# Tile t+1's first two query/key projections and first rotation issued at the end of tile t; another first tile

## The chip, the cores and the metric

The kernel runs on one core of a Trainium2 chip. Its engines run side by side, each through its own instructions in order, and wait for each other through semaphores: TensorE (PE in the profile) multiplies, VectorE (DVE), ScalarE (ACT) and GpSimd (POOL) do the rest, SyncE (SP) issues most DMAs. The metric is the device time of one execution in microseconds; lower is better.

## The reference

One transformer layer over 4096 rows of 512 numbers in float32:

```python
qkv = x @ w_qkv.T                                  # q, k, v: 16 heads of 32
q = q * cos + rotate_half(q) * sin                 # the same for k
scores = einsum('bhqd,bhkd->bhqk', q, k) * scale
keep = (rel >= 0) & (rel < 64)                     # 64 keys back at most
attn = softmax(where(keep, scores, -inf))
x1 = layernorm(x + (attn @ v) @ w_out.T)
fuse = silu((x1 @ w_gate) * s_gate) * ((x1 @ w_up) * s_up)     # 512 -> 2048, int8 weights
out = layernorm(x1 + (fuse @ w_down) * s_down)
```

## The kernel before

The rows are cut into 8 tiles of 512, a tile into 4 blocks of 128 rows. Each engine's program is written out by hand as `first()`, a loop over `body(t, True, True)` for t = 1 to 7, and `body(8, False, True)`. `first()` does the attention of tile 0 alone; `body(t)` does the attention of tile t together with the feed-forward part (FFN) of tile t-1; the last body is the FFN of tile 7.

The attention of a tile begins with three projections for each block j: "even" and "odd" query/key columns (`project_even`, `project_odd`) and values (`project_v`), each 4 float32 products of 128x512 on TensorE, written to one PSUM bank each. The first tile uses banks 0 to 3 for all of them, so that a block's projections wait until VectorE is through with those of an earlier block. VectorE rotates (`rope_products`, 4 instructions, and `rope_sums`, 2), ScalarE rounds the result to float16 (`split_high`), VectorE takes the rest as a second float16 (`split_low`; for block 3 of the first tile GpSimd does this), and SyncE turns both by DMA transposes (`turn_qk`, two for each block) into `qkT`. Values are split in the same way (`keep_v` on ScalarE, `split_v` on VectorE) and copied (`cross_v`).

Then come 16 steps s, one for each block and group of 4 heads: `scores` (TensorE), `maxima` and `bias` (VectorE), `exponentials` (ScalarE), `weights` (VectorE), `keep_probs_high` (ScalarE), `split_probs` (GpSimd), `turn_probs` (a DMA transpose), `weigh_v` (TensorE), and for every second step `keep_o` (VectorE). In the first tile a pair of buffers takes the split probabilities, so step s's `keep_probs_high` waits until the transpose of step s-2 has landed. Output projections (`project_o`), the residual and the first layer norm (`start_x1`, `finish_x1`, with the power of -0.5 on GpSimd in `invert_deviation1`) and the split of x1 for the FFN (`split_x1_high`, `split_x1`, `turn_x1`) follow.

In `body` TensorE first makes the projections in the order E0 O0 E1 O1 V0 E2 O2 V1 E3 O3 V2 (E even, O odd, V values, with the block), then two groups of scores and V3, then the 16 gate and up products of the FFN with the steps of the attention between them, the output projections, and 4 `down` products. VectorE ends a body with the second layer norm (`start_y`, `finish_y`); before that it finds the largest x of the next tile (`tile_maximum`), which GpSimd spreads over the partitions (`spread_maximum`), and works out the next tile's scales (`next_scales`). It begins the next body with the keys that are carried over, the scaled rotation tables (`start_tables`) and the rotation of block 0.

The FFN's weights come in nine DMAs from GpSimd during the first tile's steps: eight of 512 KB after the odd steps, and `wd`, 2048 KB, after the last step. The rows of x for the residual are loaded at steps 12 to 15 (`load_rows`), the next tile's x at step 6 (`load_xT`). Ahead of `first()` VectorE takes the maxima of the query/key weights and of x for the scales, in three reductions of 2048 columns.

## Time and profile before

| | |
|---|---|
| median of 3 runs | 1273.59 us (1273.41 to 1275.9) |
| the profiled execution | 1274.88 us, its span 1273.0 us |
| TensorE busy | 1203.5 us, 95% of the span, 8200 matrix products |
| VectorE busy | 932.7 us, 73% |
| ScalarE busy | 570.1 us, 45% |
| GpSimd busy | 372.7 us, 29% |
| mean granted clock of TensorE | 0.972 of full speed |

The span is the time from the first to the last instruction of the profiled execution; 1.9 us lie around it. Busy time is the time in which an engine computes; waits, branches and the issue of DMAs are not counted. The granted clock is a share of 2.4 GHz; it has two levels, 1 and 0.5, and a mean between them tells how long each was held.

### The profile page before, as it was taken

The page shows a single profiled execution, that of the slowest core. Times are in us where ns is not written, and L with a number is a line of the kernel's source. Part 1 is how long each engine was busy: PE and PEld are TensorE (multiplying, and loading weights), DVE is VectorE, ACT ScalarE, POOL GpSimd, SP SyncE. Part 2 cuts the span into 40 slices and gives each one's busy share as a digit, 9 for nine tenths or more (in the row PEclk, how much of TensorE's full clock was granted, in tenths as well). Part 3 has the DMA queues.
Part 4 walks back from the last instruction along what each step waited for, and adds up shares of the span by engine and source line. Part 5 has one row for each costly group of instructions (what it writes and reads, how often), then busy time and mean ns, then how long its engine had stood idle before and what let it go on. Part 6 is the DMA issues. An engine that isn't in the chain of part 4 may idle for free.

```text
span 1273.0 us, 24755 instructions
## 1 busy us (share of the span) xinstructions
PE 1203.5 (95%) x8200; PEld 554.6 (44%) x8200; DVE 932.7 (73%) x2794; ACT 570.1 (45%) x1609; POOL 372.7 (29%) x379
## 2 busy tenths in 40 slices
PE   7726699999999999999999999999999999999997
PEld 3312344444444444444444444444444444444443
DVE  6655589866897579965898669975799658975543
ACT  1355048801685028820487016840288105960230
POOL 0044205611154103521055102541045210551331
PEclk9857899999999999999999999999999999999999
DMA  6577665432654245550744326542545507443000
GB/s 215 116 158 179 149 132 100 99 74 67 144 105 89 51 104 121 101 96 35 150 92 92 71 75 148 102 89 44 124 104 100 94 35 165 85 84 75 25 1 33
DMA packets 346392, 124.74 MB, mean 98 GB/s; under 512 B 309536, under 2 KB 330272, under 8 KB 346272
## 3 DMA queue, kind: packets, MB, share of 16 engines
q1 hardware_dynamic: 338160, 108.32, 41.6%
q0 software_dynamic: 3216, 6.29, 1.8%
q10 hardware_dynamic: 4896, 8.52, 1.8%
q8 instruction: 76, 1.25, 0.4%
q14 instruction: 44, 0.36, 0.1%
HBM read 27.67 MB, written 8.39 MB: 28 GB/s over the span
## 4 chain that ended last, share of the span: by engine, by line
PE 86%; DVE 4%; issue 3%; DMA 2%; SPq 2%; ACT 1%; POOL 1%; POOLq 0%; ACTq 0%; DVEq 0%
PE bank L493 59%; PE bank L603 15%; PE bank L511 8%; PE bank L570 3%; PE bank L550 2%; DMA x<-y 2%; DVE fuse L831 1%; ACT bank L735 1%; DMA xT_sb<-xT 1%; SPq L313 0%; SPq L335 0%; DVE fuse L842 0%; POOL y L418 0%; POOL fuse L440 0%; SPq L296 0%
## 5 line engine op out<-in xcount | busy, mean ns | idle before, releaser
L418 POOL TENSOR_TENSOR xT_sb<-probs,xT_sb 128x512 f16<-128x512 f32 x112 | 129.6, 1157 | 413.0 <-ACT xT_sb L693 413.0
L493 PE MATMUL bank<-x1T,wg 128*128 128x512 f16 (+1 forms) x1032 | 244.2, 380 | 2.2 <-DVE ffn_tmp L890 2.2
L735 ACT ACTIVATE bank<-bank,neg_max,qk_scale 128x128 f32<-128x128 f32 x512 | 219.8, 430 | 51.7 <-DVE neg_max L883 51.7
L493 PE MATMUL bank<-x1T,wu 128*128 128x512 f16 x1024 | 241.9, 379 | 0.0
L693 ACT ACTIVATE fuse<-fuse 128x512 f16<-128x512 f32 x128 | 70.0, 617 | 378.4 <-DVE fuse L837 378.4
L493 PE MATMUL bank<-wqkv,xT_sb 128*128 128x512 f32 x512 | 229.1, 598 | 2.0 <-DMA wqkv<-w_qkvT 2.0
L603 PE MATMUL bank<-wd,fuse 128*128 128x512 f16 x1024 | 222.3, 379 | 0.0
L423 POOL TENSOR_TENSOR fuse<-ffn_tmp,fuse 128x512 f16<-128x512 f32 x128 | 148.4, 1159 | 71.5 <-ACT fuse L693 70.2
L603 PEld LDWEIGHTS bank<-wd,fuse 128*128 128x128 f16 x1024 | 100.1, 98 | 123.2 <-issue 4.0
L493 PEld LDWEIGHTS bank<-x1T,wu 128*128 128x128 f16 x1024 | 100.2, 98 | 120.9 <-issue 0.5
L493 PEld LDWEIGHTS bank<-wqkv,xT_sb 128*128 128x128 f32 x512 | 97.2, 191 | 122.5 <-issue 118.4
L493 PEld LDWEIGHTS bank<-x1T,wg 128*128 128x128 f16 x1032 | 96.6, 98 | 118.7 <-issue 5.6
L511 PE MATMUL bank<-wqkv,xT_sb 128*128 128x512 f32 x256 | 120.4, 615 | 13.4 <-DVE v_own L847 8.1
L877 DVE CUSTOM_DVE_ANT_0 bank<-bank,mask_tile 128x128 f32<-128x128 f32 x496 | 129.0, 323 | 0.0
L703 ACT ACTIVATE ffn_tmp<-bank,tanh_scale 128x512 f32<-128x512 f32 x128 | 88.1, 689 | 78.1 <-PE bank L493 46.7
L493 PE MATMUL bank<-wout,v_own 128*128 128x512 f32 x256 | 121.3, 628 | 0.8 <-DVE v_own L867 0.8
L894 DVE SCALAR_TENSOR_TENSOR ffn_tmp<-bank,fuse_scale,ffn_tmp 128x512 f32<-128x512 f32 x128 | 96.2, 751 | 19.0 <-PE bank L493 6.7
L890 DVE SCALAR_TENSOR_TENSOR ffn_tmp<-ffn_tmp,bank 128x512 f32<-128x512 f32 x128 | 86.9, 679 | 27.3 <-ACT ffn_tmp L703 27.3
L735 ACT ACTIVATION_READ_ACCUMULATOR bank<-bank,neg_max,qk_scale 128x1 f32 x512 | 104.5, 204 | 0.0
L831 DVE TENSOR_TENSOR fuse<-bank,tables 128x512 f32<-128x512 f32 x128 | 79.4, 684 | 13.7 <-PE bank L493 10.7
L842 DVE TENSOR_TENSOR fuse<-fuse 128x512 f16<-128x512 f32 x124 | 77.3, 687 | 15.2 <-ACT fuse L693 15.2
L859 DVE SCALAR_TENSOR_TENSOR probs<-bank,inv_sum 128x512 f32<-128x512 f32 x120 | 83.0, 691 | 4.8
(109 smaller groups left out, 1101.1 us busy)
## 6 DMA issues: line engine op xcount, KB each, us to landing
xT_sb<-xT SPq DMA_DIRECT2D x36, 256.0 KB, 3.9
v_cross<-v_own SPq DMA_DIRECT2D x64, 128.0 KB, 2.7
qkT<-x SPq DMA_DIRECT2D x32, 256.0 KB, 3.6
out<-y ACTq DMA_DIRECT2D x32, 256.0 KB, 2.1
wqkv<-w_qkvT SPq DMA_DIRECT2D x2, 1024.0 KB, 7.3
wg<-w_gate POOLq DMA_DIRECT2D x4, 512.0 KB, 4.2
wu<-w_up POOLq DMA_DIRECT2D x4, 512.0 KB, 4.1
wd<-w_down POOLq DMA_DIRECT2D x1, 2048.0 KB, 11.6
```

The costliest lines, as they stand in the source:

```text
L418: done(probs_low, pool.tensor_tensor(place[:, 1, :, :], probs_place(s, ffn), place[:, 0, :, :], ALU.subtract))
L423: done(fuse_low, pool.tensor_tensor(fuse[:, s, 1, :], ffn_tmp[:, s % 2, :], fuse[:, s, 0, :], ALU.subtract))
L493: last = pe.matmul(dst, lhsT, rhs, start=(i == 0), stop=(i == len(pairs) - 1))
L511: pe.matmul(even, xT_sb[:, j, k, :], wqkv[:, k, 0:EMB], start=(k == 0), stop=(k == KC - 1))
L603: last = pe.matmul(bank32[DOWN_BANKS[j % 2]], fuse[:, s, z, rows], wd[:, s, :], start=(s == 0 and z == 0), stop=(s == STEPS - 1 and z == 1))
L703: done(tanh_done, act.activation(ffn_tmp[:, s % 2, :], bank32[2 * (s % 2)], ACT.Tanh, scale=tanh_scale[:, s:s + 1]))
L735: last = act.activation(unit, unit, ACT.Exp, bias=neg_max[:, s % 2, h // 3, h % 3:h % 3 + 1], scale=qk_scale[:, 2:3], accum_out=row_sum[:, ...
L831: last = dve.tensor_tensor(free_view(rope_t[i], heads), free_view(src, heads), table(i), ALU.mult)
L859: done(probs_ready, dve.scalar_tensor_tensor(out=probs_place(s, ffn), in0=units, scalar=2.0 ** PROB_BITS, in1=inverse, op0=ALU.mult, op1=A ...
L877: last = dve.tensor_tensor_reduce(out=unit, in0=unit, in1=mask[:, :], scale=1.0, scalar=MASKED, op0=ALU.add, op1=ALU.max, accum_out=row_ma ...
L890: done(gated, dve.scalar_tensor_tensor(out=tmp, in0=tmp, scalar=1.0, in1=bank32[2 * (s % 2)], op0=ALU.add, op1=ALU.mult))
L894: done(fused, dve.scalar_tensor_tensor(out=tmp, in0=bank32[2 * (s % 2) + 1], scalar=fuse_scale[:, s:s + 1], in1=tmp, op0=ALU.mult, op1=ALU ...
```

## The change

It has four parts. First, the projections E0, O0, E1, O1 of tile t+1 stand at the end of body t instead of at the start of body t+1, as do the carried keys, the tables and the rotation of block 0 (VectorE: `carry_keys`, `first_rope`), ScalarE's `split_high` of block 0 and the load of the tables. The loop runs over t = 1 to 6; body 7 is written out, without the next tile's maximum, its spreading, its scales and its loads. Second, `first()` spreads its projections over all eight banks, rotates block 1 into the free `x1`, makes only V0 before the scores of step 0, and puts V1 to V3 into the steps. GpSimd takes `split_low` of blocks 1, 2 and 3. Step s weighs values for step s-3 instead of s-2. Third, tile 1's E0, O0, E1, O1 stand at steps 10, 11, 14 and 15 of `first()`, the first layer norm of blocks 0 and 1 at steps 9 to 15, and tile 1's keys, tables and rotation of block 0 at its end; rows of x are loaded at step 5, the next x at step 7. The FFN's weights are issued in three DMAs (2048 KB each) when the transpose of step 15 has landed. Fourth, ahead of `first()` the maxima are taken piece by piece as the loads land (four reductions of 512 columns, one of 2048, four of 512), and the FFN's constants are prepared later.

```diff
@@
-        QKV_BANKS = 4
         V_BANKS = (4, 6, 5, 7)
+        FIRST_QK_BANKS = ((2, 3), (0, 1), (5, 6), (2, 3))
+        FIRST_V_BANKS = (7, 0, 1, 3)
+        FIRST_PROJ_BANKS = (2, 3, 6, 5)
         DOWN_BANKS = (5, 7)
...
+            return bank32[(V_BANKS if ffn else FIRST_V_BANKS)[j]]
+
+        def proj_bank(j, ffn):
+
+            return bank32[j if ffn else FIRST_PROJ_BANKS[j]]
 
...
-            with eng.Fori(1, NT) as t:
-                body(t, True, True)
-            body(NT, False, True)
+            with eng.Fori(1, NT - 1) as t:
+                body(t, True, True, True)
+            body(NT - 1, True, True, False)
...
-                cross_v(a, 1)
-                turn_qk(a, 2)
                 for s in range(STEPS):
                     turn_probs(a, s, False)
                     if s == 0:
-                        cross_v(a, 2)
-                    if s == 4:
+                        turn_qk(a, 2)
+                    if s in (2, 5):
+                        cross_v(a, (1, 2)[s // 5])
+                    if s == 6:
                         turn_qk(a, 3)
+                    if s == 5:
+                        for j in range(NB):
+                            load_rows(a, j)
+                    if s == 7:
                         cross_v(a, 3)
-                    if s == 6:
                         for j in range(NB):
                             load_xT(a + 1, j, False)
-                    if s >= STEPS - NB:
-                        load_rows(a, s - (STEPS - NB))
-
-            def body(t, attn, ffn):
+                    if s == 8:
+                        load_tables(a + 1)
+
...
-                    for j in range(NB):
-                        load_xT(a + 1, j)
+                    if more:
+                        for j in range(NB):
+                            load_xT(a + 1, j)
+                        load_tables(a + 1)
...
-                a = 0
+                a, ffn = 0, False
+                split_low(a, 1, ffn)
                 for s in range(STEPS):
-                    split_probs(a, s, False)
-                    if s % 2:
-                        load_inner(*((w_gate, wg) if s < 2 * KC else (w_up, wu)), s // 2 % KC)
-                    if s == 3:
-                        split_low(a, 3)
+                    split_probs(a, s, ffn)
+                    if s == 0:
+                        split_low(a, 2, ffn)
+                    if s == 5:
+                        split_low(a, 3, ffn)
+                    if s in (10, 14):
+                        invert_deviation1(a, s // 4 - 2)
+                pool.wait_ge(first_probsT_in[NB - 1], 16 * STEPS // NB)
+                for src, dst in ((w_gate, wg), (w_up, wu)):
+                    pool.dma_start(dst[:, :, :], src.rearrange("(k p) n -> p k n", p=P)).then_inc(wffn_in, 16)
                 pool.dma_start(wd[:, :, :], w_down.rearrange("(s p) n -> p s n", p=P)).then_inc(wffn_in, 16)
-                for j in range(NB):
+                for j in range(2, NB):
...
+            def project_even(a, j, ffn, early=False):
 
                 wait_xT(pe, a, j)
-                if ffn:
+                if early:
+                    wait(*((v_low, pe, a - 1, 1) if j == 0 else (proj_read, pe, a - 1, 0)))
+                elif ffn:
                     wait(*((proj_read, pe, a - 1, 2 * j + 1) if j < 2 else (rope_read, pe, a, j - 2)))
-                elif j >= 2:
-                    wait(v_low, pe, a, j - 2)
+                elif j == NB - 1:
+                    wait(rope_read, pe, a, 0)
...
+            def project_odd(a, j, ffn, early=False):
+
+                if early:
+                    wait(*((v_low, pe, a - 1, 2) if j == 0 else (proj_read, pe, a - 1, 1)))
+                if j == 0 and not ffn:
+                    pe.wait_ge(wq_odd_in, 16)
                 done(qk_done, qkv(j, 1, qk_banks(j, ffn)[1]))
...
-                for j in range(NB - 1):
+                for j in range(2):
                     project_even(a, j, ffn)
                     project_odd(a, j, ffn)
-                    project_v(a, j, ffn)
+                project_v(a, 0, ffn)
+                project_even(a, 2, ffn)
+                project_odd(a, 2, ffn)
                 scores(a, 0, ffn)
+                project_even(a, 3, ffn)
+                project_odd(a, 3, ffn)
                 scores(a, 1, ffn)
-                project_even(a, 3, ffn)
                 scores(a, 2, ffn)
-                project_odd(a, 3, ffn)
-                for s in range(STEPS):
-                    if 1 <= s < STEPS - 2:
+                project_v(a, 1, ffn)
+                for s in range(1, STEPS):
+                    if s + 2 < STEPS:
                         scores(a, s + 2, ffn)
-                    if s == 1:
+                    if s >= 3:
+                        weigh_v(a, s - 3, ffn)
+                    if s == 3:
+                        project_v(a, 2, ffn)
+                    if s == 6:
                         project_v(a, 3, ffn)
-                    if s >= 2:
-                        weigh_v(a, s - 2, ffn)
-                    if s in (8, 12, 15):
-                        project_o(a, (s - 7) // NG if s < 15 else 2, ffn)
+                    if s in (8, 12):
+                        project_o(a, s // 4 - 2, ffn)
+                    if s in (10, 14):
+                        project_even(a + 1, s // 4 - 2, True, True)
+                    if s in (11, 15):
+                        project_odd(a + 1, s // 4 - 2, True, True)
+                weigh_v(a, STEPS - 3, ffn)
+                project_o(a, 2, ffn)
                 weigh_v(a, STEPS - 2, ffn)
                 weigh_v(a, STEPS - 1, ffn)
                 project_o(a, NB - 1, ffn)
 
-            def body(t, attn, ffn):
+            def body(t, attn, ffn, more):
                 a, f = t, t - 1
 
                 if attn:
-                    for j in range(NB):
+                    project_v(a, 0, ffn)
+                    for j in range(2, NB):
                         project_even(a, j, ffn)
                         project_odd(a, j, ffn)
-                        if j:
-                            project_v(a, j - 1, ffn)
+                        project_v(a, j - 1, ffn)
...
                     down(f, j, attn)
+                if more:
+                    for j in range(2):
+                        project_even(a + 1, j, ffn)
+                        project_odd(a + 1, j, ffn)
...
+                split_high(a, 0, ffn)
+                split_high(a, 1, ffn)
+                exponentials(a, 0)
                 keep_v(a, 0, ffn)
-                keep_v(a, 1, ffn)
-                split_high(a, 2)
-                exponentials(a, 0)
-                keep_v(a, 2, ffn)
+                split_high(a, 2, ffn)
                 for s in range(1, STEPS):
                     exponentials(a, s)
                     keep_probs_high(a, s - 1, ffn)
-                    if s == 2:
-                        split_high(a, 3)
-                    if s == 3:
-                        keep_v(a, 3, ffn)
+                    if s in (2, 4, 8):
+                        keep_v(a, s.bit_length() - 1, ffn)
+                    if s == 5:
+                        split_high(a, 3, ffn)
+                    if s == 12:
+                        split_x1_high(a, 0)
                 keep_probs_high(a, STEPS - 1, ffn)
-                split_x1_high(a)
-
-            def body(t, attn, ffn):
+                split_x1_high(a, 1)
+                split_high(a + 1, 0, True)
+                split_x1_high(a, 2)
+                split_x1_high(a, 3)
...
+            def carry_keys(a):
+                wait(scale_chain, dve, a - 1, 7)
+                wait_qkT(dve, a - 1, NB - 1)
+                done(k_carried, dve.tensor_scalar(before, qkT[:, NB, :, WINDOW:P], carry_scale[:, :], None, ALU.mult))
+
+            def first_rope(a):
+                start_tables(a)
+                rope_products(a, 0, True)
+                rope_sums(a, 0, True)
+
...
+                    if s >= 5 and s % 2:
+                        keep_o(a, (s - 5) // 2)
                     attention_step(a, s, ffn)
-                    if s == 1:
+                    if s == 3:
                         rope_products(a, 3, ffn)
-                        rope_sums(a, 3)
-                    if s == 3:
-                        split_v(a, 3, ffn)
+                        rope_sums(a, 3, ffn)
+                    if s in (2, 5, 8):
+                        split_v(a, (s + 1) // 3, ffn)
+                    if s in (9, 13):
+                        start_x1(a, s // 4 - 2, ffn)
+                    if s in (11, 15):
+                        finish_x1(a, s // 4 - 2)
+                    if s == 14:
+                        split_x1(a, 0)
+                next_scales(a, ffn)
+                carry_keys(a + 1)
                 keep_o(a, STEPS // 2 - 2)
+                first_rope(a + 1)
+                split_x1(a, 1)
                 keep_o(a, STEPS // 2 - 1)
+                dve.wait_ge(v_setup, V_SETUP_STEPS + 1)
+                start_x1(a, 2, ffn)
+                finish_x1(a, 2)
+                start_x1(a, 3, ffn)
+                split_x1(a, 2)
+                finish_x1(a, 3)
+                split_x1(a, 3)
+                dve.reciprocal(fuse_inv[:, :], power[:, 2:3]).then_inc(fuse_inverted, 1)
                 dve.wait_ge(sdown_in, 16)
                 dve.tensor_scalar(sdown[:, :], sdown[:, :], power[:, 2:3], 2.0 ** 18, ALU.mult, ALU.mult)\
                     .then_inc(sdown_scaled, 1)
...
-                split_v(a, 0, ffn)
-                split_v(a, 1, ffn)
-                rope_products(a, 2, ffn)
...
                 finish_y(f, NB - 1)
+                if more:
+                    carry_keys(a + 1)
+                    first_rope(a + 1)
...
+            for k in range(KC):
+                dve.wait_ge(wq_even_in[k], 16)
+                dve.tensor_reduce(part_max[:, k:k + 1], wqkv[:, k, 0:EMB], AX.X, ALU.max,
+                                  apply_absolute_value=True).then_inc(setup, 1)
+            dve.wait_ge(wq_odd_in, 16)
+            dve.tensor_reduce(part_max[:, KC:KC + 1], wqkv[:, :, EMB:2 * EMB], AX.XY, ALU.max,
+                              apply_absolute_value=True).then_inc(setup, 1)
+            for j in range(NB):
+                wait_xT(dve, 0, j)
+                dve.tensor_reduce(x_max[:, j:j + 1], xT_sb[:, j, :, :].rearrange("p k t -> p (k t)"), AX.X, ALU.max,
+                                  apply_absolute_value=True).then_inc(setup, 1)
+            dve.wait_ge(setup, SETUP_MAXIMA - 2)
+            dve.tensor_reduce(largest[:, 0:1], x_max[:, :], AX.X, ALU.max).then_inc(setup, 1)
+            dve.tensor_reduce(largest[:, 1:2], part_max[:, :], AX.X, ALU.max).then_inc(setup, 1)
+            count[0] += 2
...
```

TensorE in `first()`, from the program's first product; `bank` with a number is the PSUM bank written, `wqkv,xT_sb` is a projection, `qkT` a group of scores. Before:

```order
L511 MATMUL bank0<-wqkv,xT_sb 128x512 x4
L493 MATMUL bank1<-wqkv,xT_sb 128x512 x4
L493 MATMUL bank2<-wqkv,xT_sb 128x512 x4
L511 MATMUL bank3<-wqkv,xT_sb 128x512 x4
L493 MATMUL bank0<-wqkv,xT_sb 128x512 x4
L493 MATMUL bank1<-wqkv,xT_sb 128x512 x4
L511 MATMUL bank2<-wqkv,xT_sb 128x512 x4
L493 MATMUL bank3<-wqkv,xT_sb 128x512 x4
L493 MATMUL bank0<-wqkv,xT_sb 128x512 x4
L550 MATMUL bank4<-qkT 32x128 x16
L550 MATMUL bank6<-qkT 32x128 x16
L511 MATMUL bank1<-wqkv,xT_sb 128x512 x4
```

And of the change, the same place:

```order
L534 MATMUL bank2<-wqkv,xT_sb 128x512 x4
L514 MATMUL bank3<-wqkv,xT_sb 128x512 x4
L534 MATMUL bank0<-wqkv,xT_sb 128x512 x4
L514 MATMUL bank1<-wqkv,xT_sb 128x512 x4
L514 MATMUL bank7<-wqkv,xT_sb 128x512 x4
L534 MATMUL bank5<-wqkv,xT_sb 128x512 x4
L514 MATMUL bank6<-wqkv,xT_sb 128x512 x4
L578 MATMUL bank4<-qkT 32x128 x16
L534 MATMUL bank2<-wqkv,xT_sb 128x512 x4
L514 MATMUL bank3<-wqkv,xT_sb 128x512 x4
L578 MATMUL bank6<-qkT 32x128 x16
```

The scores of step 0 (the first row with `qkT`) stand behind seven projections instead of nine, and no bank is used twice ahead of them.

TensorE at steps 10 to 12 of the first tile; `v_cross` and `v_own` are the two halves of `weigh_v`, `wout` is an output projection. Before:

```order
L550 MATMUL bank6<-qkT 32x128 x16
L570 MATMUL bank7<-x1,v_cross 32x128 x8
L570 MATMUL bank7<-x1,v_own 32x128 x8
L550 MATMUL bank5<-qkT 32x128 x16
L570 MATMUL bank7<-x1,v_cross 32x128 x8
L570 MATMUL bank7<-x1,v_own 32x128 x8
L493 MATMUL bank1<-wout,v_own 128x512 x4
L550 MATMUL bank4<-qkT 32x128 x16
L570 MATMUL bank7<-x1,v_cross 32x128 x8
```

And of the change:

```order
L578 MATMUL bank4<-qkT 32x128 x16
L598 MATMUL bank7<-x1,v_cross 32x128 x8
L598 MATMUL bank7<-x1,v_own 32x128 x8
L534 MATMUL bank0<-wqkv,xT_sb 128x512 x4
L578 MATMUL bank6<-qkT 32x128 x16
L598 MATMUL bank7<-x1,v_cross 32x128 x8
L598 MATMUL bank7<-x1,v_own 32x128 x8
L514 MATMUL bank1<-wqkv,xT_sb 128x512 x4
L578 MATMUL bank5<-qkT 32x128 x16
L598 MATMUL bank7<-x1,v_cross 32x128 x8
L598 MATMUL bank7<-x1,v_own 32x128 x8
L514 MATMUL bank3<-wout,v_own 128x512 x4
```

The two rows with `wqkv,xT_sb` are E0 and O0 of tile 1, each between the scores or weighed values of two steps.

VectorE at the end of `first()`, from `keep_o` of steps 14 and 15 on; `v_own<-bank` is `keep_o`, `fuse<-bank,tables` are `rope_products`. Before:

```order
L867 TENSOR_REDUCE v_own<-bank 128x256 x2
L1028 TENSOR_SCALAR sdown<-sdown,power 128x512
L900 SCALAR_TENSOR_TENSOR qkT<-bank,v_scale,qkT 128x512
L905 BN_STATS stats<-qkT 128x6
L907 MEMSET wait_taker 128x1
L908 BN_AGGR mean_var<-stats 128x2
L910 TENSOR_SCALAR mean_var<-mean_var 128x1
```

And of the change, from the carried keys on:

```order
L1052 TENSOR_SCALAR qkT<-qkT,carry_scale 128x16x64
L918 TENSOR_REDUCE v_own<-bank 128x256
L1032 TENSOR_SCALAR tables<-tables,qk_scale 128x256
L881 TENSOR_TENSOR fuse<-bank,tables 128x512 x4
L887 TENSOR_TENSOR fuse<-fuse 128x512
L888 TENSOR_TENSOR fuse<-fuse 128x512
L978 SCALAR_TENSOR_TENSOR qkT<-qkT 128x512
L918 TENSOR_REDUCE v_own<-bank 128x256
L952 SCALAR_TENSOR_TENSOR qkT<-bank,first_unscale,qkT 128x512
```

The carried keys, the tables and tile 1's rotation of block 0 stand around the last two `keep_o`; before, they stood 43 rows behind the last `keep_o`, inside the loop.

## Rows read from the trace of the kernel before

**Rows 1.** Page, the chain that ended last: share of the span by engine.

```profile
PE 86%; DVE 4%; issue 3%; DMA 2%; SPq 2%; ACT 1%; POOL 1%; POOLq 0%; ACTq 0%; DVEq 0%
```

**Rows 2.** Busy time by stretch (us: stretch and length; busy and count by engine; clock; DMA).

```profile
61.40:138.80 77.40, 32.83 (x485) 16.60 (x487) 38.92 (x185) 37.96 (x139) 28.38 (x29) 0.68 0.81 190
...
293.30:441.00 147.70, 147.70 (x1026) 68.19 (x1025) 114.94 (x346) 71.13 (x201) 44.63 (x46) 1.00 0.45 95
```

**Rows 3.** TensorE's timeline, first tile, front (start, length, what, idle before it).

```profile
41.05 5.69 PE L511 MATMUL bank<-wqkv,xT_sb 128*128 128x512 f32 x8 [8.11 <-DVE v_own L847]
```

**Rows 4.** VectorE's timeline, first tile, front.

```profile
16.78 2.28 DVE L1143 TENSOR_REDUCE largest<-xT_sb 128x1 f32<-128x2048 f32 x1
...
22.40 2.48 DVE L831 TENSOR_TENSOR fuse<-bank,tables 128x512 f32<-128x512 f32 x4
...
60.75 0.69 DVE L859 SCALAR_TENSOR_TENSOR probs<-bank,inv_sum 128x512 f32<-128x512 f32 x1
```

**Rows 5.** Page, groups of instructions: a group of maxima (count; busy us, mean ns; idle).

```profile
L877 DVE CUSTOM_DVE_ANT_0 bank<-bank,mask_tile 128x128 f32<-128x128 f32 x496 | 129.0, 323 | 0.0
```

**Rows 6.** The chain in order of time, front.

```profile
6.06 7.92 DMA xT_sb<-xT
```

**Rows 7.** DMA issues by line: count, KB each, median us from issue to landing.

```profile
wg<-w_gate POOLq DMA_DIRECT2D x4, 512.0 KB, 4.2
...
wd<-w_down POOLq DMA_DIRECT2D x1, 2048.0 KB, 11.6
...
qkT<-fuse SPq DMA_TRANSPOSE x64, 4.0
```

**Rows 8.** TensorE's timeline, steps and end of the first tile, start of tile 1.

```profile
67.17 0.30 PE L570 MATMUL bank<-x,v_cross 128*32 128x128 f16 x8 [1.11 <-DMA x<-y]
...
103.71 0.29 PE L570 MATMUL bank<-x,v_cross 128*32 128x128 f16 x8 [1.76 <-DMA x<-y]
...
120.20 0.29 PE L570 MATMUL bank<-x,v_cross 128*32 128x128 f16 x8 [0.89 <-DVE v_own L867]
...
138.78 0.40 PE L570 MATMUL bank<-x,v_cross 128*32 128x128 f16 x8 [8.62 <-DMA x<-y]
...
155.95 7.03 PE L493 MATMUL bank<-wqkv,xT_sb 128*128 128x512 f32 x16
...
191.16 0.41 PE L550 MATMUL bank<-qkT 128*32 128x128 f16 x16
```

**Rows 9.** The timelines of GpSimd and of SyncE's issues, first tile.

```profile
76.83 4.48 POOL L440 TENSOR_TENSOR fuse<-fuse 128x512 f16<-128x512 f32 x4
...
83.86 5.98 SPq L313 DMA_TRANSPOSE qkT<-fuse  x2
```

**Rows 10.** The chain in order of time: two transposes of probabilities.

```profile
109.89 2.89 DMA x<-y
...
128.31 10.42 DMA x<-y
```

**Rows 11.** VectorE's timeline, start of tile 1 and of tile 2.

```profile
147.35 0.75 DVE L900 SCALAR_TENSOR_TENSOR qkT<-bank,v_scale,qkT 128x512 f32<-128x512 f32 x1
...
160.35 2.50 DVE L842 TENSOR_TENSOR fuse<-fuse 128x512 f16<-128x512 f32 x4 [0.70 <-ACT fuse L693]
...
308.92 2.50 DVE L842 TENSOR_TENSOR fuse<-fuse 128x512 f16<-128x512 f32 x4 [0.69 <-ACT fuse L693]
...
335.34 0.75 DVE L847 SCALAR_TENSOR_TENSOR v_own<-bank,v_scale,v_own 128x512 f16<-128x512 f32 x1
```

**Rows 12.** TensorE's timeline behind the last looped tile.

```profile
1184.62 1.89 PE L493 MATMUL bank<-x1T,wu 128*128 128x512 f16 x8
1188.71 3.50 PE L493 MATMUL bank<-x1T,wg 128*128 128x512 f16 x8 [2.20 <-DVE ffn_tmp L890]
```

**Rows 13.** The timelines of VectorE and GpSimd behind the last looped tile.

```profile
1161.49 0.15 DVE L910 TENSOR_SCALAR mean_var<-mean_var 128x1 f32<-128x1 f32 x1
...
1173.37 0.59 POOL L482 TENSOR_TENSOR rstd<-mean_var,half_power 128x1 f32<-128x1 f32 x1 [7.67 <-issue]
```

212 lines of the change are left out of this document (98 added, 114 removed).

## The prediction

> **What bounds the kernel now.** I read the chain first: TensorE holds 86% of the span [rows 1], so a stage gains only where TensorE stops. The stretches say where. From tile 1 on it never stops: in tile 2's period it is busy for 147.70 of 147.70 us at clock 1.00 [rows 2], and TensorE's list of waits has none between 146 and 1188. In the first tile's steps it is busy for 32.83 of 77.40 us, at a mean clock of 0.68 [rows 2]: each step goes through six engines' work and a DMA transpose, and the reader is to see that nothing is full there. So the change can gain in three places: ahead of the first tile's steps, in these steps, and behind the last looped tile.
>
> One moment measures the first two: the start of tile 1's V0, the first product that follows the moved ones in both kernels. Before, the row of 16 records at 155.95 is O1 and V0, 3.43 us each [rows 8], so V0 starts at 155.95 + 3.43 = 159.4. I call it T.
>
> **Front, to the first weights (60.75 + 0.69 = 61.44 before [rows 4]).** Three reductions of 2.2 us stand ahead of the scales; the last ends at 19.06 [rows 4]. Taken piece by piece they run under the loads, and the last piece waits for the last load of x, landed at 6.06 + 7.92 = 13.98 [rows 6]. A quarter of 2.28 us (0.6) and two tiny reductions (some 0.4) bring 15.0, so 4.1 us earlier. The memset of the carried keys and the two FFN constants also leave the path, 0.5 us together, an estimate from their sizes. The first rotation then starts at 22.40 - 4.6 = 17.8.
>
> Behind it, before, VectorE stood still: TensorE waited 8.11 us for `split_v` to free a bank, and ran its next eight records in 5.69 us instead of 3.43, since the clock had fallen [rows 3]. With eight banks no such wait is left, and TensorE's seven projections end at about 32. So VectorE's own list decides: 22 instructions of 0.6 us (2.48 for 4 [rows 4]) for three rotations and `split_low` of block 0, one `split_v` of 0.7, two reductions of 2.2, two groups of maxima of 4 x 0.32 [rows 5] with their small bias, the value scales at about 1.2 (8 tiny instructions), the weights at 0.9, and about 1 us of waits between dependent ones: 23.8 us. The only foreign wait is the scores of step 0. `split_low` of block 0 ends 8.3 us behind the rotation's start, at 26.1; the second transpose is issued 1.5 us or more later and lands in 4.0 [rows 7], so at 31.6, and VectorE reaches the maxima at 32.0. Hidden, but by 0.4 us only; if the two issues take the 5.98 us of [rows 9], it costs up to 1.5 us. `split_low` of block 1 goes to GpSimd at 4.48 us [rows 9] and lies beside VectorE. The first weights end at 17.8 + 23.8 = 41.6: **19.8 us earlier**.
>
> **The steps.** Before, step 0 weighs values 67.17 - 61.44 = 5.7 us behind the first weights, so now at 47.3. Step 15 came at 138.78 [rows 8]: 15 steps in 71.6 us. Steps 7 to 12 show an undisturbed pace: 103.71 to 120.20 is 16.5 us for five, with an output projection in it, 3.3 each [rows 8]. At that pace 15 steps take 49.5; seven early ones took 36.5 instead of 23.1 (block 3's split on GpSimd, 4.48, its two transposes on SyncE, 5.98 [rows 9], four loads of x and four weight pieces), and the last three took 18.6 instead of 9.9: there a transpose took 10.42 us where an undisturbed one took 2.89 [rows 10], with the last weight piece and `wd` on the DMA engines. In the change no weight is loaded in the steps, which takes the last excess away. But two blocks (2 and 3) are now split on GpSimd and turned by SyncE in the steps, and SyncE also issues four row loads, four loads of x and the tables. GpSimd's queue behind a split is the next step's `split_probs`, so its 4.48 us show. Bounds: 49.5 + 2 x 4.5 at best, if SyncE's part hides, less what the deeper pipeline (s-3) hides of a split, 57.7 in all; at worst both splits, two times 5.98, six us for nine loads and one us for each early projection of tile 1 (3.43 us warm, 5.69 cold, in steps where TensorE idles half the time): 49.5 + 9.0 + 12.0 + 6 + 4 = 80. I take 65: 5 for the first block, 8 for the second with the loads (before, 13.4 with one split, and with weights), 2.5 for the projections. Step 15 comes at 112.3, **6.6 us gained**.
>
> **From step 15 to T.** Before, 159.4 - 138.78 = 20.6: the step, `keep_o`, an output projection at the low clock, and E0, O0, E1, O1 at 3.43 each, 13.7. Now these four are gone. `keep_o` stands behind the tables, the rotation and one split of x1 (4.5 us), which begin with step 14, so it is some 2 us late; the projection after it finds a warmer clock. I take 7.0 for the rest, against 6.9 before: T = 119.3, **13.6 us gained**. Up to T the sum is 19.8 + 6.6 + 13.6 = 40.0.
>
> **Tile 1.** TensorE then needs block 2's split values at the scores of step 2, at 191.16 [rows 8], 31.8 behind V0. VectorE's work from `split_low` of block 0 to `split_v` of block 2 takes 336.1 - 308.9 = 27.2 [rows 11]. Before, it began 160.35 - 159.4 = 1.0 behind V0 [rows 11], 3.6 to spare. Now the last layer norm of the first tile, two splits, and the FFN constants stand ahead of it in VectorE's queue: from 147.35 to the scales at 153.0 [rows 11] such a remainder took 5.6, so it begins about 5 behind T and ends at 32.2: 0.4 late, and step 0's weights, next on VectorE, hold the scores of step 3. Between 0 and 5; I take **2.0 lost**. Tiles 2 to 7 keep TensorE's order, and VectorE's too but for the place of the loop's branch; I count them at nothing, since TensorE waits nowhere there, and the cover is those 3.6 us.
>
> **Behind tile 7.** TensorE stops at 1186.35 and goes on at 1188.71, with 3.50 us for eight records that take 1.89 [rows 12]: 4.0 in all. It waits for step 0's gating, which stands behind four outputs on ScalarE. GpSimd is late: the deviation that VectorE has ready at 1161.64 is inverted at 1173.37 [rows 13], since the spread maximum stands between. Body 7 has no spread now, so the outputs follow the `down` products; the last one ends at 1179.5, VectorE, GpSimd and gating need about 5.5 behind it, 1185.0: before TensorE asks. **3.8 us gained**; if another wait follows, 0.
>
> Sum: 40.0 - 2.0 + 3.8 = 41.8 on the profiled execution's 1274.88, which is 1.3 above the median. On the median 1273.59 that is 1231.8; I say **1232**.
>
> **The DMA queues at T.** The weights, 6144 KB, are issued when step 15's transpose lands, 7 us ahead of T. 512 KB land in 4.2 us, 2048 in 11.6 [rows 7]: each further 512 KB costs 7.4 / 3 = 2.5 us, which makes 31 for all, or 7.4 / 4 = 1.85, 24.5 for all, since `wd` had a piece ahead of it. The gate of step 0 needs them 28 us behind T, and they are there 17.5 to 24 behind it: hidden. What they delay is SyncE's queue: four transposes of x1 and block 0's two, needed by the scores 24 us behind T. The row says that a transpose beside such a load hardly moves, 10.42 against 2.89 [rows 10]; then the six start when the weights end and need about 8 us (4.0 to the first landing [rows 7]; 0.8 for each of the others is my estimate): there at 25.5 to 32, so 1.5 to 8 late. I take 1.5, and count it within the 2.0 of tile 1, since the two waits lie over each other. The Trainium skill ("DMA: Bandwidth & Descriptors", Queues, rings and completion order) says that each DMA engine takes turns between the queues, packet by packet. By that the transposes go on beside the weights, nothing is late, and the sum would be 0 to 1.5 us better; the row speaks against it.
>
> **Rivals.** *Weights starve the transposes* (15%): as above, with 31 us for the weights the scores are 8 us late and ScalarE's next split behind them, 10 lost in place of 2: 1240. For it, the 10.42; against it, the piece ahead of `wd`. *The steps stay slow* (20%): the loads and the two blocks cost as much as weights did, 73 to 80 us, 1240 to 1247. For it, 36.5 us for seven steps. *Faster steps* (12%): 58, with no loss in tile 1: 1223. *Every looped tile gains a wait* (3%, slower): if the new place of the branch, or SyncE's table load, made TensorE wait in tiles 2 to 7, six times, it would take 7 us each to use up 41.8; only 3.6 are spare in VectorE's queue, but no row shows a wait of that kind. At 8 us a tile: 1280. *The change does nothing* (2%): the steps' chain would have to give back all of the front; at 1273.
>
> **How the numbers follow.** Forecast 48%, by its own bounds 1226 to 1238. With the faster steps at 1223 and the slow steps and starved transposes up to 1247, the range is 1222 to 1247; outside it lie the two last rivals and both slow ones together. Two tenths of a percent, 2.5 us, is about what a measurement tells from no change. Faster 0.95, same 0.02, slower 0.03.
>
> **What would show it.** T at 115 to 123 in TensorE's timeline; the first weights of VectorE at 41 to 43; step 15 weighed about 65 us behind step 0; no transpose over 6 us in the steps; the gap behind the last looped tile gone; 147.7 us a tile as before. Wrong if TensorE waits in tile 1 for more than 5 us on `qkT` or x1's transpose, or if the steps take 75 us.

## The result, and the profile after

The changed kernel takes **1241.15 us**, the median of 4 runs (1240.21 to 1242.04), against 1274.32 us for the kernel before (4 runs, 1273.41 to 1275.90). The ratio is 0.9738, 95% interval 0.9721 to 0.9755: 33.2 us faster, where the sum said 41.8. The profiled execution took 1242.04 us with a span of 1240.2 us, 32.8 less than the span of before.

The busy time by stretch of the changed kernel: the first tile's steps, and tile 2's period (columns as in [rows 2]); the last row is the kernel before, over the same 15 steps.

```profile
51.00:117.40 66.40, 49.48 (x484) 22.27 (x475) 44.09 (x182) 33.90 (x118) 25.13 (x24) 0.78 0.76 142
273.00:420.70 147.70, 147.70 (x1025) 68.23 (x1024) 116.17 (x349) 71.19 (x201) 45.07 (x45) 1.00 0.50 95
...
67.20:138.80 71.60, 28.14 (x444) 14.66 (x447) 33.23 (x167) 34.03 (x123) 25.43 (x27) 0.66 0.83 195
```

Tile 2 is as before: 147.70 us, all of it TensorE's. In the 15 steps TensorE is busy for 49.48 of 66.40 us instead of 28.14 of 71.60, at a mean clock of 0.78 instead of 0.66. (The row of 77.40 us in [rows 2] starts earlier, at the first weights.)

TensorE's timeline of the changed kernel, from the first scores into tile 1. A projection shows as 3.6 or 3.7 us at clock 1 and as more where part of it ran at 0.5.

```profile
33.51 0.41 PE L578 MATMUL bank<-qkT 128*32 128x128 f16 x16 [1.67 <-DMA qkT<-fuse]
...
50.72 0.41 PE L598 MATMUL bank<-x,v_cross 128*32 128x128 f16 x8 [1.25 <-DMA x<-y]
...
85.44 0.62 PE L578 MATMUL bank<-qkT 128*32 128x128 f16 x16 [4.47 <-DMA qkT<-fuse]
...
89.12 6.24 PE L534 MATMUL bank<-wqkv,xT_sb 128*128 128x512 f32 x8 [1.92 <-DMA xT_sb<-xT]
...
117.28 0.28 PE L598 MATMUL bank<-x,v_cross 128*32 128x128 f16 x8
...
120.55 5.40 PE L514 MATMUL bank<-wout,v_own 128*128 128x512 f32 x8 [2.88 <-DVE v_own L918]
125.79 3.60 PE L514 MATMUL bank<-wqkv,xT_sb 128*128 128x512 f32 x8
...
151.03 0.41 PE L578 MATMUL bank<-qkT 128*32 128x128 f16 x16 [0.71 <-DVE v_own L898]
...
159.10 0.41 PE L578 MATMUL bank<-qkT 128*32 128x128 f16 x16 [0.57 <-DVE v_own L898]
...
165.12 0.41 PE L578 MATMUL bank<-qkT 128*32 128x128 f16 x16 [1.71 <-DVE probs L910]
...
173.23 0.29 PE L598 MATMUL bank<-xT_sb,v_cross 128*32 128x128 f16 x8 [0.36 <-DMA xT_sb<-xT_sb]
```

The row at 125.79 is V0 of tile 1, the moment T: 33.6 us sooner than before (159.4). Step 0 weighs values at 50.72 and step 15 at 117.28, so 15 steps take 66.6 us (71.6 before). Behind T stand four short waits, 3.35 us together, that before did not exist. They are at the scores of steps 1, 2 and 4 and at the first weighed values. After 173.23 TensorE waits only once more, 0.50 us at 1107.74 in the written-out body.

VectorE's timeline of the changed kernel, front:

```profile
18.10 2.48 DVE L881 TENSOR_TENSOR fuse<-bank,tables 128x512 f32<-128x512 f32 x4
...
33.97 0.29 DVE L928 CUSTOM_DVE_ANT_0 bank<-bank,mask_start 128x128 f32<-128x128 f32 x1 [1.55 <-issue]
...
36.15 1.17 DVE L1183 TENSOR_TENSOR v_scale<-qk_scale,v_ratio 128x2 f32<-128x2 f32 x1
...
39.98 1.22 DVE L887 TENSOR_TENSOR fuse<-fuse 128x512 f32<-128x512 f32 x1
41.13 0.68 DVE L888 TENSOR_TENSOR fuse<-fuse 128x512 f32<-128x512 f32 x1
...
43.87 0.69 DVE L910 SCALAR_TENSOR_TENSOR probs<-bank,inv_sum 128x512 f32<-128x512 f32 x1
```

GpSimd's timeline beside it has one row between 30 and 45 us, `split_low` of block 1:

```profile
36.15 4.50 POOL L457 TENSOR_TENSOR fuse<-x,fuse 128x512 f16<-128x512 f32 x4 [6.95 <-issue]
```

The first weights end at 43.87 + 0.69 = 44.56, 16.9 us sooner than before [rows 4]. The row of two elements for each partition that takes 1.17 us (0.16 before), and the sum that takes 1.22 instead of 0.68, lie beside GpSimd's split.

TensorE's timeline behind the last looped tile shows the gap of [rows 12] closed: one row follows the other, with no idle time.

```profile
1150.30 1.91 PE L514 MATMUL bank<-x1T,wg 128*128 128x256 f16 x16
1152.04 1.89 PE L514 MATMUL bank<-x1T,wu 128*128 128x512 f16 x8
```

The balance by these moments: T 33.6 us sooner; from T to the first gate of the last body 1150.30 - 125.79 = 1024.5 us, against 1020.0 before, so 4.5 lost (4.0 in tile 1, 0.5 at 1107.74); behind it 3.7 gained. 33.6 - 4.5 + 3.7 = 32.8.

### The profile page after: what moved, and what is told of

Its sections match the earlier page's. It is cut to its first block, busy times and chain, and to the rows that moved or that the text cites. A ratio compares the mean times of both kernels' runs of the same rounds, so it can differ in the third digit from the quotient of the medians.

```text
span 1240.2 us, 24503 instructions
## 1 busy us (share of the span) xinstructions
PE 1198.2 (97%) x8200; PEld 551.6 (44%) x8200; DVE 926.6 (75%) x2782; ACT 570.1 (46%) x1609; POOL 377.6 (30%) x380
## 4 chain that ended last, share of the span: by engine, by line
PE 81%; DVE 7%; issue 5%; ACT 2%; DMA 2%; SPq 2%; POOL 1%; POOLq 0%; DVEq 0%; ACTq 0%
PE bank L514 52%; PE bank L631 17%; PE bank L534 7%; PE bank L598 2%; PE bank L578 2%; ACT bank L778 1%; SPq L328 1%; DVE fuse L881 1%; DVE bank L928 1%; DMA xT_sb<-xT_sb 1%; DMA wqkv<-w_qkvT 1%; ACT fuse L736 1%; DMA x<-y 1%; DVE probs L910 1%; DVE row_max L928 0%
## 5 line engine op out<-in xcount | busy, mean ns | idle before, releaser
L514 PE MATMUL bank<-wout,v_own 128*128 128x512 f32 x256 | 116.4, 607 | 2.9 <-DVE v_own L918 2.9
L893 DVE TENSOR_TENSOR fuse<-fuse 128x512 f16<-128x512 f32 x116 | 72.3, 686 | 19.9 <-ACT fuse L736 19.9
## 6 DMA issues: line engine op xcount, KB each, us to landing
wu<-w_up POOLq DMA_DIRECT2D x1, 2048.0 KB, 12.6
```

What stands on the lines that cost most here:

```text
L514: last = pe.matmul(dst, lhsT, rhs, start=(i == 0), stop=(i == len(pairs) - 1))
```

## The experiments

All of them are in a stand-in form: each transposing DMA is an ordinary DMA of 256-byte pieces, so nothing is transposed and the output is another one. The first two show what the form is worth as a base.

### The bases

```diff
-                    sp.dma_start_transpose(qkT[:, slot, :, :], split_flat[...])
+                    sp.dma_start(qkT[:, slot, :, :], free_view(split_flat[...], [[P // 2, 16], [1, P]]))
```

and likewise for the weights of a step and for x1. Of the kernel before:

> A stand-in for the kernel before, as a base for the experiments: each transposing DMA is an ordinary DMA of as many 256-byte pieces into the same tile on the same queue, so nothing is transposed and the output is another one; all instructions of the engines, all waits and all other transfers stay. If ordinary transfers land about as soon as the transposing ones (3 to 5 us after issue), the time is 1265 to 1280 us and the stand-in can take the place of the kernel before. Rival: they land 1 to 2 us sooner and issue sooner; then the steps of the first tile, which are a chain through one transfer each, shorten from 4.8 to 3.5 or 4 us and the time is 1250 to 1262 us.

Of the changed kernel:

> The same stand-in for the changed kernel. Theory (the gain is in the order of the work, not in how the transposing transfers run): 25 to 35 us less than the stand-in of the kernel before. Rival (the gain hangs on the transfers, with weights no longer loaded between the steps, and the stand-ins escape that): 10 to 20 us less.

Measured: 1271.39 us (10 runs, 1268.43 to 1275.13; ratio to the kernel before 0.9978, 0.9962 to 0.9993) and 1240.64 us (4 runs, 1237.65 to 1240.94; ratio 0.9734, 0.9715 to 0.9754). The difference is 30.8 us; the gain does not hang on the transposing transfers. The changed kernel's stand-in has T at 125.41 instead of 125.79, and the same waits of 2.87, 0.70, 0.57 and 1.71 us. The stand-in of before is less faithful: its profiled steps are 6 us shorter, and most of that has a reason that comes below ("Ahead of the weights or behind them").

Two cautions for small differences. The kernel before, run beside each group of experiments, had medians of 1274.20, 1274.09, 1274.76 and 1275.96 us. So medians of different groups can be off by up to 1.9 us against each other; the ratios, which are to the kernel before in the same group, are not. And five kernels with the same front as the changed kernel's stand-in, that stand-in among them, end their first weights anywhere between 44.06 and 45.08 us, so a single trace does not show a change of 1 us there.

### The two halves of the change alone

First the new first tile without the move and the written-out body:

```diff
-                    if s in (10, 14):
-                        project_even(a + 1, s // 4 - 2, True, True)
-                    if s in (11, 15):
-                        project_odd(a + 1, s // 4 - 2, True, True)
...
-                carry_keys(a + 1)
                 keep_o(a, STEPS // 2 - 2)
-                first_rope(a + 1)
                 split_x1(a, 1)
```

> Stand-in form (its bases: 1271.4 us before, 1240.6 us changed). The new first tile (banks, order, rows, weights at its end) without the move: tile 1's two projections, scales and first rotation stand at the start of its body as before, and the last body is a round of the loop as before. Theory A (the four projections fill waits of TensorE inside the first tile's steps, so that they cost nothing there): the steps stay at 4.4 us, tile 1's V projection of block 0 starts 13 to 16 us later than in the changed kernel (139 to 142 us against 125.4), the tail keeps its gap, and the time is 1255 to 1260 us. Rival B (the projections push the steps apart by as much as they take): the steps shorten to 3.5 to 4.0 us, and the time is 1243 to 1249 us. Rival C (the first tile's own reorder is worth nothing, the projections in the steps give all): 1268 us or more.

Measured: 1245.03 us (5 runs; ratio 0.9770, 0.9755 to 0.9786). By time this is rival B, but the pace of the steps (4.2 us) is neither theory's. TensorE's timeline of this kernel:

```profile
50.32 0.41 PE L595 MATMUL bank<-x,v_cross 128*32 128x128 f16 x8 [0.94 <-DMA x<-y]
...
113.33 0.28 PE L595 MATMUL bank<-x,v_cross 128*32 128x128 f16 x8
...
114.53 3.70 PE L513 MATMUL bank<-wout,v_own 128*128 128x512 f32 x8 [0.80 <-DVE v_own L905]
```

The 15 steps take 63.0 us, against 65.8 in the base (51.14 to 116.91): the four projections cost 2.8 us inside the steps. The last output projection waits 0.80 us and runs at clock 1, 3.70 us, where the changed kernel waits 2.88 us and needs 5.40: 3.8 us more that the move costs. The last of the four projections starts at 128.36 and V0 3.43 us later, at 131.8, 6.4 later than with the move, though step 0 came 0.8 sooner in this run: 13.7 - 2.8 - 3.8 - 0.8 = 6.3. And tile 1 loses nothing: from V0 to the last body's first gate (1151.96) are 1020.2 us, as before the change, against 1023.8 in the base. So the move gives 6.4, costs 3.6 in tile 1, and its written-out body gives 1.4 at the tail (this kernel waits 1.41 there): 4.2, and 4.4 is the difference of the medians. Theory A had the missing 13.7 us of projections right, but neither their price in the steps, nor the wait at the last output sum, nor tile 1's. The new first tile alone gives 26.4 us of the 30.8 by the medians.

Then the move without the new first tile, and of the move only the written-out last body:

```diff
-            with eng.Fori(1, NT) as t:
-                body(t, True, True)
+            with eng.Fori(1, NT - 1) as t:
+                body(t, True, True, True)
+            body(NT - 1, True, True, False)
...
-                    spread_maximum(a)
+                    if more:
+                        spread_maximum(a)
```

> Stand-in form. The kernel before with the move alone: projections of blocks 0 and 1, scales, tables and first rotation at the tile's end, the last attention tile written out without a next one; the first tile is as before, so its four projections still follow its last output projection. Theory: TensorE's order is the same as before, so only the tail gives, 1.2 to 3.8 us (its gap is 1.2 us in the stand-in of before and 3.5 us in the kernel before): 1267.5 to 1270.5 us. Rival: the loop's jump now stands between the first rotation and the second on VectorE instead of ahead of the carried keys, and each of seven tiles gains up to 3 us: 1247 to 1255 us. Second rival: the tables and the scales come at a worse time and each tile loses 1 us or more: over 1275 us.

> Stand-in form. The kernel before with the last attention tile written out, without the maximum, its spread over the partitions, the scales and the loads for a tile that isn't there; nothing else is moved. Theory (the tail's gap is the spread that stands ahead of the square roots on GpSimd): the last body's waits are gone, as in the move alone: 1267.5 to 1270.5 us, within 1 us of it. Rival (the gap goes only when the order of the scales changes too): the gap stays, 1271 to 1272 us.

Measured: 1269.77 us (7 runs; ratio 0.9963, 0.9948 to 0.9978) and 1269.54 us (10 runs; ratio 0.9956, 0.9939 to 0.9972), 1.6 and 1.9 below their base. The intervals overlap the base's, so the times alone do not show a gain; the trace of the second does. Its last body starts with

```profile
1180.52 1.91 PE L499 MATMUL bank<-x1T,wg 128*128 128x256 f16 x16
1182.26 1.89 PE L499 MATMUL bank<-x1T,wu 128*128 128x512 f16 x8
```

and has no idle time, where the base waits 1.22 us and the kernel before 2.20 with a row at the low clock behind it [rows 12]. So the written-out body closes the gap. It leaves out the maximum, its spread, the scales and the loads together; that the spread is the one that counts is read from GpSimd's timeline [rows 13] and not tested by itself. The move adds nothing of its own in seven tiles: from V0 to the last body are 1019.8 us in the move-only kernel and 1021.3 in the other, so the loop's branch at another place costs nothing that shows.

### Weights back in the steps

```diff
                     split_probs(a, s, ffn)
+                    if s % 2:
+                        load_inner(*((w_gate, wg) if s < 2 * KC else (w_up, wu)), s // 2 % KC)
...
-                pool.wait_ge(first_probsT_in[NB - 1], 16 * STEPS // NB)
-                for src, dst in ((w_gate, wg), (w_up, wu)):
-                    pool.dma_start(dst[:, :, :], ...)
```

> Stand-in form of the changed kernel (1240.6 us) with one part undone: gate and up weights are loaded in eight pieces by GpSimd behind every second step, as in the kernel before, and the down weights behind the last step. Theory (the prediction's: a load on the other queue beside a 256-byte transfer keeps it from moving, 10.42 us instead of 2.89): the 15 steps take 71 to 73 us instead of 66, T comes at 130 to 132 instead of 125.4, and the time is 1245 to 1248 us. Rival (the changed kernel's steps have other waits that cover the pieces): less than 2 us more, 1241 to 1242.5.

Measured: 1245.13 us (5 runs; ratio 0.9764, 0.9750 to 0.9779), 4.5 more than the base; V0 at 129.77, 4.4 later; the 15 steps take 71.3 us (50.11 to 121.43), 5.5 more, of which an earlier step 0 has 1.0. The rival falls, and the theory stands at its lower end (V0 just ahead of its 130). The transfers are what got slower: the 16 of the probabilities land after 4.8 us by the median, 3.1 in the base, and the four of the queries and keys in the steps after 8.8 instead of 6.6. The other thing that the edit brings, GpSimd's own 0.57 us for each issue, stands once on the chain that ends last in these steps, for 0.51 us at 71.82. So the slowing is smaller than the theory's 10.42 for 2.89, and spread over many transfers.

### Ahead of the weights or behind them

The runs above also tell why the kernel before lost so much at step 15 [rows 10]. Each has the same 2048 KB load of `wd` at the end of the steps. In the move-only kernel GpSimd issues it ahead of SyncE's transfer of step 15; in the stand-in of before and in the kernel just above the two come within 0.5 us, the transfer first. The timelines of SyncE and GpSimd, and what TensorE then waited, in the move-only kernel:

```profile
127.18 1.19 POOL L464 DMA_DIRECT2D wd<-w_down  x1
...
128.15 0.60 SPq L305 DMA_DIRECT2D x<-y  x1
...
138.10 0.40 PE L578 MATMUL bank<-x,v_cross 128*32 128x128 f16 x8 [8.54 <-DMA x<-y]
```

In the stand-in of the kernel before:

```profile
126.34 0.92 SPq L303 DMA_DIRECT2D x<-y  x1
...
126.40 1.19 POOL L462 DMA_DIRECT2D wd<-w_down  x1
...
132.64 0.40 PE L573 MATMUL bank<-x,v_cross 128*32 128x128 f16 x8 [3.70 <-DMA x<-y]
```

In the kernel with the weights back in the steps:

```profile
116.32 0.59 SPq L318 DMA_DIRECT2D x<-y  x1
...
116.76 1.19 POOL L484 DMA_DIRECT2D wd<-w_down  x1
...
121.43 0.29 PE L603 MATMUL bank<-x,v_cross 128*32 128x128 f16 x8 [0.17 <-DMA x<-y]
```

A transfer issued 1.0 us behind the weights is used 10.0 us after its issue; one issued 0.06 or 0.44 us ahead of them, 6.3 and 5.1 us after. Two more traces agree. The kernel with only the last body written out issues the weights at 126.60 and the transfer at 127.46, and uses it at 137.72, 10.3 us after. The kernel before does so at 126.64 and 128.31, and its transpose takes the 10.42 us of [rows 10]. That the pieces here are ordinary ones shows that transposing is not the reason. No run exchanges the two issues and nothing else, so the order as the cause is read from these five traces, not tested. The nearest pair is the stand-in of before and the kernel with only the last body written out, whose programs up to there are alike: 3.7 us against 8.6 of waiting. It may be why the stand-in's runs lie 6.7 us apart, too, but which run had which order is not known.

### Three whole maxima instead of nine pieces

```diff
-            for k in range(KC):
-                dve.wait_ge(wq_even_in[k], 16)
-                dve.tensor_reduce(part_max[:, k:k + 1], wqkv[:, k, 0:EMB], ...)
+            for k in range(KC):
+                dve.wait_ge(wq_even_in[k], 16)
+            dve.tensor_reduce(part_max[:, 0:1], wqkv[:, :, 0:EMB], ...)
```

(the maxima of x likewise)

> Stand-in form of the changed kernel with one part undone: the maxima of the weights and of x are three whole reductions that wait for all their loads, instead of nine pieces. Theory: the first rotation starts 3.5 to 4.5 us later (22 instead of 18.1), and all of it is kept: T at 129 to 130, 1244 to 1245 us. Rival (TensorE's first projections and the transfers of the step 0 are late in any case, since the first scores already wait 1.4 us for a transfer): less than 2 us.

Measured: 1241.43 us (5 runs; ratio 0.9734, 0.9718 to 0.9750): 0.8 more than the base, with the same ratio. The theory falls. VectorE's timeline of this kernel:

```profile
8.42 2.29 DVE L1203 TENSOR_REDUCE part_max<-wqkv 128x1 f32<-128x2048 f32 x1 [6.26 <-DMA wqkv<-w_qkvT]
...
14.01 2.29 DVE L1210 TENSOR_REDUCE x_max<-xT_sb 128x1 f32<-128x2048 f32 x1 [0.49 <-DMA xT_sb<-xT]
...
18.79 1.89 DVE L884 TENSOR_TENSOR fuse<-bank,tables 128x512 f32<-128x512 f32 x3
```

VectorE's timeline of the kernel before has, as the first thing ahead of its three reductions:

```profile
11.65 0.23 DVE L1126 CAST mask_start<-y 128x128 bf16<-128x128 f32 x1 [10.13 <-DMA ffn_tmp<-s_up]
```

So the three reductions were late because they stood behind the masks and the FFN's constants, which could not start before 11.65. Freed of that, whole reductions run under the loads as well (the last ends at 16.3 us, the last piece of the changed kernel at 15.6), and the pieces add 0.7 us at most (the rotation at 18.79 here, 18.66 in its base, 18.10 in the changed kernel).

### SyncE: block 3 ahead of the rows

```diff
                     if s == 5:
+                        turn_qk(a, 3)
+                    if s == 6:
                         for j in range(NB):
                             load_rows(a, j)
-                    if s == 6:
-                        turn_qk(a, 3)
...
-                    if s in (9, 13):
+                    if s in (10, 13):
                         start_x1(a, s // 4 - 2, ffn)
```

> Stand-in form of the changed kernel; SyncE issues block 3's two transfers of split queries and keys right behind step 5's transfer, ahead of step 6's and of the four row loads (which follow step 6), and block 0's output is added to x one step later. Theory (the scores of step 12 wait 4.32 us at 85.75 because these two stand behind the rows): they start 3 to 4 us sooner, and T comes 2 to 3.5 us sooner: 1237.2 to 1238.7 us. Rival (the wait goes to the next one in the chain, step 6's or 7's transfer of the split weights, which now stands behind them): within 0.7 us of 1240.6.

Measured: 1242.19 us (5 runs; ratio 0.9742, 0.9727 to 0.9757), 1.5 more than the base, within the intervals, so not faster. TensorE's timeline:

```profile
83.28 0.41 PE L601 MATMUL bank<-x,v_cross 128*32 128x128 f16 x8 [5.05 <-DMA x<-y]
...
88.54 0.41 PE L601 MATMUL bank<-x,v_cross 128*32 128x128 f16 x8 [4.21 <-DMA x<-y]
```

The wait of 4.32 us for block 3 is gone, and step 6 now waits 5.05 us for its own transfer, issued behind block 3's two, where it waited 2.25; step 7 waits 4.21 instead of 0.83. V0 comes 1.0 later. This is the rival: the place in SyncE's queue does not remove a wait there, it chooses whose it is.

### The output sum first, constants early, value scales early

Three edits in VectorE's list, each on top of the base or of the one before it:

```diff
-                first_rope(a + 1)
-                split_x1(a, 1)
+                start_tables(a + 1)
+                rope_products(a + 1, 0, True)
                 keep_o(a, STEPS // 2 - 1)
+                rope_sums(a + 1, 0, True)
+                split_x1(a, 1)
```

> Stand-in form of the changed kernel (1240.6 us), with the first tile's last sum of weighed values (the one that block 3's output projection waits for) put right behind tile 1's first rotation products, ahead of their sums and of the low half of x1 of block 1. Theory: the wait of 2.87 us at 120.18 shrinks to about 1.0 us, the projection stays warm (3.7 instead of 5.4 us), V of tile 1 starts 3 to 3.6 us earlier, and 2 to 3.6 us of it are kept: 1237.0 to 1238.7 us. Rival (tile 1 then waits for the rotation that comes 0.7 us later and for x1 of block 3, which is bound by VectorE and GpSimd, not by TensorE): within 0.7 us of 1240.6, with the waits of tile 1 grown by as much.

Measured: 1237.78 us (5 runs; ratio 0.9713, 0.9697 to 0.9729), 2.9 less than the base. The time lies in the theory's range, but the intervals overlap (the base has 0.9715 to 0.9754), so the trace has to decide. TensorE's timeline:

```profile
117.58 3.70 PE L517 MATMUL bank<-wout,v_own 128*128 128x512 f32 x8 [0.93 <-DVE v_own L921]
121.12 3.60 PE L517 MATMUL bank<-wqkv,xT_sb 128*128 128x512 f32 x8
...
147.39 0.41 PE L581 MATMUL bank<-qkT 128*32 128x128 f16 x16 [1.73 <-DVE v_own L901]
147.73 5.40 PE L517 MATMUL bank<-wqkv,xT_sb 128*128 128x512 f32 x8
```

The wait falls from 2.87 to 0.93 and the projection runs at clock 1: from step 15 to V0 it is 4.9 us instead of 8.5, 3.6 sooner. V0 comes 4.3 sooner, but 0.9 of that is a sooner step 0, which this edit does not touch. From V0 to the last body 2.1 are given back; most visible are 1.73 + 5.40 here for 0.70 + 3.70 in the base.

Then the constants (reciprocal, `sdown`, `fuse_scale`) from the end of the first tile to step 7:

> The fourth experiment (output sum first, 1237.8 us, in which tile 1 gave back 2 of 4.3 us) with the three instructions for the FFN constants moved from the end of the first tile to step 7, where VectorE idles. Theory (what is lost in tile 1 is VectorE's queue): its split of tile 1's block 0 starts 1.0 us sooner, and TensorE's waits behind T shrink by 0.9 to 1.7 us: 1236.1 to 1236.9 us. Rival (tile 1 is held by the inversions on GpSimd or by transfers): no change, 1237.4 to 1238.2.

Measured: 1237.39 us (5 runs; ratio 0.9708, 0.9692 to 0.9724), 0.4 less, within the intervals: the rival. V3 runs at clock 1 again and the first gate comes at 151.19 instead of 152.96, but then TensorE waits 0.57 and 1.72 us at the scores of steps 2 and 4, as in the base; from T to the last body it is 1025.5 us here and 1025.9 without this edit. ScalarE's timeline of this kernel says which half of the rival it is:

```profile
143.44 2.19 ACT L739 ACTIVATE fuse<-fuse 128x512 f16<-128x512 f32 x4 [5.22 <-DMA qkT<-fuse]
```

This is `split_high` of block 2 in tile 1, and it waits until block 0's two transfers have landed. They are issued from 130.38 on, beside the FFN's weights, and land 11.2 us after their issues by the median. VectorE's split of block 0 does start 1.0 us sooner (127.39 for 128.38), and then VectorE waits for this row. It is the same in the kernel without this edit (143.51) and in the best version (142.59); in the changed kernel's stand-in ScalarE waits for VectorE instead.

Last the value scales, on the base alone and on top of the two others:

```diff
+                first_v_scale()
                 maxima(a, 0)
                 bias(a, 0)
-                first_v_scale()
```

> Stand-in form of the changed kernel (1240.6 us) with VectorE's eight tiny instructions for the value scales put ahead of the maxima of step 0, into the 1.4 us in which VectorE waits for the first scores. Theory (the front's 3 us of lateness against the prediction are this uncovered wait, and GpSimd's split of block 1 at 36.8 slows what follows on VectorE): the first weights end 1.2 to 2.2 us sooner, 42.9 to 43.9 instead of 45.1, and T comes as much sooner: 1238.4 to 1239.6 us. Rival (the steps have other waits, block 1's transfers at 48.6 and the order of GpSimd's splits, that take it back, as they took back the 0.95 us of the whole maxima): the first weights sooner, T within 0.5 us of 125.4, 1240.2 to 1241.2 us. Second rival (the scales wait for GpSimd's spread themselves and hold the maxima): the first weights as late as before.

> The eighth experiment (output sum first, FFN constants in step 7; 1237.4 us) with the value scales ahead of the maxima of step 0 too: the best version so far. If the front's gain is kept: 1235.2 to 1236.4 us; if the steps take it back: 1237.0 to 1237.9 us.

Measured: 1239.92 us (5 runs; ratio 0.9720, 0.9706 to 0.9733) and 1237.09 us (5 runs; ratio 0.9698, 0.9683 to 0.9713). VectorE's timeline of the first of them:

```profile
33.99 0.16 DVE L1186 TENSOR_TENSOR v_scale<-qk_scale,v_ratio 128x2 f32<-128x2 f32 x1
...
38.27 1.57 DVE L890 TENSOR_TENSOR fuse<-fuse 128x512 f32<-128x512 f32 x1
39.76 1.64 DVE L891 TENSOR_TENSOR fuse<-fuse 128x512 f32<-128x512 f32 x1
...
43.45 0.69 DVE L913 SCALAR_TENSOR_TENSOR probs<-bank,inv_sum 128x512 f32<-128x512 f32 x1
```

The scales fit into the wait at 0.16 us apiece. The first weights end 0.9 us sooner than in the base (44.14 against 45.08), less than the 1.2 to 2.2 expected and within what kernels with an equal front differ by. GpSimd's split lies beside VectorE as in the base, on the rotation's two sums (1.57 and 1.64 us; 1.47 and 1.64 there). Step 0 weighs its values at 51.55, not sooner than the base's 51.14, so the 2.0 us by which V0 comes sooner (123.39) are not the front's: the 15 steps take 63.4 us. They take 63.8 in the best version, and 65.1 to 66.1 in four stand-ins without this edit (the base, whole maxima, the output sum first, the constants early); why is open. Neither theory foresaw this. The last body comes 1.4 sooner; the medians differ by 0.7 us and the ratios (0.9720 and 0.9734) by 1.8, with overlapping intervals, so this edit alone is inconclusive. The three together are 3.6 us below the base by the medians and 4.6 by the ratios, and the intervals (0.9683 to 0.9713, and 0.9715 to 0.9754) do not meet: this is the best version, in the stand-in form; with transposing transfers it was not run.

## Why the prediction was right, and where it was off

The time, 1241.15 us, lies in the stated range but 3 us outside the forecast's own bounds of 1226 to 1238. The range reached that far because of two rivals, slow steps and starved transposes, and neither came true; that several small misses added up to a time in their stretch is luck. The mechanism, stage by stage, was right in the main.

**Front, to the first weights: 16.9 us instead of 19.8.** The start was right, 18.10 for 17.8, and its reason mostly wrong: "taken piece by piece they run under the loads" is worth 0.7 us at most, and the rest of the 4.3 comes from what no longer stands ahead of the reductions, the masks and constants with their wait to 11.65, and behind them, 0.8 us. The prediction had only the latter, at 0.5. Of the other 12.6 us no run tells the banks from the order. By VectorE's rows, gone are its waits of 8.65 us for TensorE and 0.85 for ScalarE, two `split_low` of 2.4 and two `split_v` of 0.7, 15.7 in all; the two terms below, 1.55 and 1.5, are new. These were mis-sized. "Hidden, but by 0.4 us only" was not hidden: SyncE's two issues for block 0 took 5.08 us and VectorE waits 1.55 us at 33.97 for the first scores, the case for which the text gave up to 1.5. And GpSimd's split "lies beside VectorE" but is not free of it: 1.17 for 0.16 and 1.22 for 0.68, 1.5 us. The Trainium skill ("SBUF — State Buffer", Who interferes with whom) has VectorE and GpSimd share a pair of ports; the trace agrees so far, since the same instructions take 0.16 and 0.68 us where GpSimd is idle. Beside the same split the rotation's products, with one operand from PSUM, kept their 2.48 us for four.

**The steps: 66.6 us for 65.** Right, in parts too: the projections cost 2.8 where 2.5 was taken, and the weights' absence is worth 4.4 us at V0. For that it had the last three steps' excess in mind, 8.7 us; with the weights back, the loss lies in earlier steps too. Early steps were slow as feared: waits of 4.47 us for block 3 and 1.92 for x. Behind those, from 89.12 to 117.6, TensorE waits 0.95 us in all, so the late steps are its own work now.

**Step 15 to T: 8.5 us for 7.0.** The four projections are gone from it, 13.7 us, as said. That `keep_o` is "some 2 us late" was right: TensorE waits 2.88 us for it, 0.80 before. "A warmer clock" was not: behind that wait the projection took 5.40 us at a mean granted clock of 0.67, like the 5.62 at 0.65 before. Putting the sum first gave both back.

**Tile 1: 4.5 us lost for 2.0.** The mechanism was right, VectorE's queue, and its start too early. VectorE's timeline:

```profile
125.99 0.75 DVE L952 SCALAR_TENSOR_TENSOR qkT<-bank,first_unscale,qkT 128x512 f32<-128x512 f32 x1 [2.47 <-PE bank L514]
...
132.11 2.48 DVE L893 TENSOR_TENSOR fuse<-fuse 128x512 f16<-128x512 f32 x4
```

VectorE waits for the last output projection, which ends as V0 starts, and has block 3's layer norm to do before its split of block 0: at 132.11, T + 6.3, for the T + 5 of the text. TensorE then waits 0.71, 0.57 and 1.71 us, for block 1's and block 2's split values and for the weights of step 1; the text had looked at block 2 and at step 0's weights. The waits come from one lateness. Once the scores of step 1 wait for VectorE, those of step 2 follow 8.07 us later and those of step 4 another 6.02, the time of VectorE's list between them, and eight kernels have both intervals within 0.02 us. The loss does not come from an earlier T: with the weights back in the steps T is 4.4 later, the split starts at T + 6.3 as well and the waits are the same. It comes with the move. In the kernel without it the four projections stand between the last output projection and V0, the split starts 1.9 us ahead of V0, and nothing is lost.

**Weights at T.** The issues of the changed kernel between 112 and 142 us (the columns are of [rows 7]):

```profile
wg<-w_gate POOLq DMA_DIRECT2D x1, 2048.0 KB, 8.4
wu<-w_up POOLq DMA_DIRECT2D x1, 2048.0 KB, 12.6
wd<-w_down POOLq DMA_DIRECT2D x1, 2048.0 KB, 19.0
x1T<-qkT SPq DMA_TRANSPOSE x4, 8.1
```

The last weights land 19.0 us behind an issue at 117.72, at 136.7: T + 11, sooner than the 17.5 to 24 of the text. The first transpose of x1, issued ahead of them, lands after 3.8 us; the three issued behind them take 13.1, 9.0 and 7.2, and SyncE is held for 5.11 us by the issue of the last (1.2 to 1.3 for the others). So they are slowed, as the row of [rows 10] said, though they do move beside the weights. TensorE did not wait for them, and the 1.5 us put down to them was not seen in this kernel. It is seen where T comes sooner still: with the output sum first, ScalarE waits for block 0's transfers, as shown above, and that is what made the constants' place worth nothing. The rule of taking turns packet by packet between queues (Trainium skill, "DMA: Bandwidth & Descriptors", Queues, rings and completion order) gives by itself no reason for the difference between a transfer issued 1.0 us behind the weights and one 0.06 ahead of them, 10.0 against 6.3 us.

**Behind tile 7: 3.7 us for 3.8.** Right, and as far as tested by the cause named: the written-out body alone closes the gap.

The sum again: T 6.5 us later than forecast (3.0 in the front, 0.5 to the first weighing, 1.6 in the steps, 1.5 behind them), 2.5 more lost in tile 1, 0.1 less at the tail: 41.8 - 9.1 = 32.7, measured 32.8. All terms had their sign right, and all were too good, the tail's by least. In the front the cause is plain: the undisturbed duration of an instruction or an issue that now has more beside it. Of its own signs, T (115 to 123) and the first weights (41 to 43) came out late; of the transposes, block 2's two took 6.1 and 6.3 us, just over its 6, and those of the probabilities 5.3 at most. The steps, the gap and tile 2's period came as said. None of the rivals came true; *the steps stay slow* was nearest, with 66.6 of its 73 us.

## What to carry to other kernels

Work moved into an engine's idle time is paid where the queue next runs full: the four projections gained 13.7 us at one place and gave 2.8, 3.8 and 3.6 back in the steps, at the last output sum and in the next tile, so the queue of the engine that serves the moved work deserves as close a look as the gap it fills. In front of an early chain, look first for what stands ahead of it in program order and waits for an unrelated small load; cutting the work in pieces came second by far. Issue a latency-bound transfer ahead of a bulk load rather than behind it. And when an edit takes away a wait and nothing is gained, read what the next wait in the chain is for: here it was a transfer that had been harmless as long as VectorE was later.

## What the hardware showed beyond expectation

The order of two issues went with 4 to 5 us: a 256 KB transfer in 256-byte pieces issued 0.9 to 1.7 us behind a 2048 KB load on GpSimd's queue was used 10.0 to 10.4 us after its issue (three traces, one with transposing transfers), and 6.3 or 5.1 us after when issued 0.06 or 0.44 us ahead of it (two traces). A bulk load also holds the queue that issues beside it: behind 6144 KB of weights the issue of one transpose took SyncE 5.11 us instead of 1.24. Ordinary 256-byte pieces in place of transposing transfers changed the changed kernel by 0.5 us in 1241. And beside GpSimd's split of a block a VectorE instruction on two elements for each partition, both operands in SBUF, took 1.17 us instead of 0.16 (one trace), and sums of 128x512 took 1.22 to 1.64 instead of 0.68; a copy of one operand right behind it kept its 0.15 us.
